# A graph and attention layer on one core: the mask products cut into four 64x64 pieces, and the mask made one step sooner

## The reference

```python
xn = _layernorm(x)
# sparse attention over the edges
x_norm = _layernorm(xn, ln_g, ln_b)
q, k, v = (x_norm @ Wq + bq), (x_norm @ Wk + bk), (x_norm @ Wv + bv)     # as (N, H, HD)
scores = jnp.einsum('ehd,ehd->eh', q[origin], k[destination]) * SCALE
ws = scores * edge_weights
e = jnp.exp(ws - seg_max[origin])
att = e / (denom[origin] + 1e-16)
values = segment_sum(att[:, :, None] * v[destination], origin)
gnn = xn + (values @ W1 + b1) @ W2 + b2
# linear attention mixer on the same xn, then a small table-like block
x = x + gnn + mix(xn)
x = x + ffn(_layernorm(x))
```

## Time and profile before

| what | value |
|---|---|
| median of 3 runs | 853.5 us (851.43 to 857.59) |
| the profiled execution, device time | 854.37 us |
| its span in the trace | 851.2 us |
| busy: TensorE, VectorE, ScalarE, GpSimd | 92%, 69%, 40%, 54% of the span |
| chain that ended last, by engine | PE 70%, DVE 21%, DMA 4% |
| attention loop, from the first scores | about 365 us to the end |
| granted TensorE clock, mean | 0.98 |

### The profile page before, as it was taken

The page is one execution under the profiler, slowest core; times in us unless marked ns, Lnnn a source line. Parts: engine busy times, 40 slices in busy tenths (PEclk is TensorE's granted clock), DMA queues, the critical chain, the costliest instruction groups (busy, mean ns, idle before and its releaser), DMA issues.

```text
span 851.2 us, 13484 instructions
## 1 busy us (share of the span) xinstructions
PE 782.4 (92%) x4751; PEld 458.3 (54%) x4791; DVE 583.2 (69%) x1331; ACT 339.6 (40%) x794; POOL 457.5 (54%) x391
## 2 busy tenths in 40 slices
PE   2999897899999999979999999999999999999993
PEld 2554445444446444435555555555556667666661
DVE  3487594954233503358888888998988978878886
ACT  0311301022312122035556555556555555545662
POOL 1028878778778877777777787777610001001000
PEclk9989999998999999979999999999999999999998
DMA  7697968897546569315353535435354143242203
GB/s 225 175 375 269 320 203 277 250 357 227 161 136 200 158 185 335 95 15 193 103 202 104 185 120 160 146 103 193 108 164 165 66 152 104 95 148 89 86 1 120
DMA packets 69632, 143.98 MB, mean 169 GB/s; under 512 B 20537, under 2 KB 54251, under 8 KB 65599
## 3 DMA queue, kind: packets, MB, share of 16 engines
q1 hardware_dynamic: 47084, 119.42, 39.9%
q0 software_dynamic: 13344, 6.28, 6.6%
q10 hardware_dynamic: 9136, 17.39, 6.2%
HBM read 77.99 MB, written 64.77 MB: 168 GB/s over the span
## 4 chain that ended last, share of the span: by engine, by line
PE 70%; DVE 21%; DMA 4%; issue 3%; ACTq 1%; ACT 1%; DVEq 0%
PE bank L890 17%; PE bank L884 12%; DVE AR L1540 11%; PE bank L1118 8%; PE bank L1085 8%; PE bank L1100 8%; PE bank L1090 4%; PE bank L1147 4%; DVE AR L1549 3%; DMA AR<-w_tab 2%; PE bank L998 2%; PE bank L873 1%; DMA AR<-in_L_gnn_b_dram 1%; PE bank L987 1%; PE bank L949 1%
## 5 line engine op out<-in xcount | busy, mean ns | idle before, releaser
L514 POOL DMA_INDIRECT w_tab<-pay,idx x330 | 403.9, 1224 | 153.3 <-issue 153.0
L765 ACT ACTIVATE AR<-AR,nmx 128x512 f32<-128x512 f32 (+1 forms) x240 | 159.0, 664 | 48.0 <-DVE nmx L1544 46.5
L1540 DVE CUSTOM_DVE_ANT_0 AR<-bank,AR,MX 128x512 f32<-128x512 f32 (+1 forms) x160 | 151.8, 986 | 20.0 <-PE bank L1090 19.1
L772 ACT ACTIVATE AR<-bank 128x512 f32<-128x512 f32 (+1 forms) x120 | 67.3, 561 | 173.9 <-PE bank L1100 173.9
L1085 PE MATMUL bank<-KT,QT 64*128 64x512 f32 (+1 forms) x480 | 118.3, 570 | 8.6 <-issue 5.3
L1100 PE MATMUL bank<-ident,AR 128*128 128x128 f32 (+2 forms) x880 | 122.7, 280 | 1.1 <-ACT AR L765 1.1
L1118 PE MATMUL bank<-AR,V 128*64 128x128 f32 (+1 forms) x1600 | 114.0, 280 | 6.1 <-DVE AR L1549 6.0
L884 PE MATMUL bank<-AR 128*128 128x512 f32 (+1 forms) x288 | 109.0, 538 | 7.3 <-ACT QT L642 3.2
L1118 PEld LDWEIGHTS bank<-AR,V 128*64 128x64 f32 (+1 forms) x1600 | 85.6, 136 | 52.3 <-issue 50.9
L890 PE MATMUL bank<-AR 128*128 128x512 f32 x240 | 108.3, 607 | 2.5 <-ACT AR L696 2.5
L1100 PEld LDWEIGHTS bank<-ident,AR 128*128 128x128 f32 (+2 forms) x880 | 94.0, 139 | 22.3 <-issue 15.9
(11 more groups left out here) (250 smaller groups left out, 755.2 us busy)
## 6 DMA issues: line engine op xcount, KB each, us to landing
w_tab<-ztile SPq DMA_DIRECT2D x20, 2280.0 KB, 15.0
AR<-w_tab SPq DMA_DIRECT2D x20, 2048.0 KB
AR<-w_tab SPq DMA_DIRECT2D x10, 1344.0 KB
w_tab<-ztile SPq DMA_DIRECT2D x3, 1800.0 KB, 13.2
w_tab<-pay,idx POOLq DMA_INDIRECT x330, 4.4
w_tab<-ztile SPq DMA_DIRECT2D x2, 1700.0 KB, 16.5
kv_rows<-AR ACTq DMA_DIRECT2D x9, 256.0 KB, 6.5
kv_rows<-V ACTq DMA_DIRECT2D x9, 256.0 KB
```

The source lines that it names most:

```text
L514: pool.indirect_dma_start(out=w_tab, out_offset=bass.IndirectOffsetOnAxis(ap=idx[:, k, j:j + 1], axis=0), in_=pay[:, k % RING, j, :], in_o ...
L765: act.activation(ws[u % 2][hh][:, 0:n], ws[u % 2][hh][:, 0:n], ACT.Exp, bias=nmx[:, u % 4, hh:hh + 1], accum_out=DG[g][:, c, 2 * p + hh:2 ...
L772: act.activation(PT[u % 2][0][:, 0:nb * P], bank[2][:, 0:nb * P], ACT.Copy).then_inc(s_ea, 1)
L1540: v.tensor_tensor_reduce(out=ws[u % 2][hh][:, 0:n], in0=bank[SB[(2 * u + hh) % 3]][:, 0:n], in1=Wt[w % 2][:, 0:n, h], scale=1.0, scalar=MX ...
```

## The change

It touches four places. On TensorE the mask of one head is now two products of 64x64 instead of one of 128x128, four for the two heads of a unit. The even head uses the rows 0 to 63 of the array, the odd head the rows 64 to 127, each once for the lower and once for the upper half of the output partitions. Two of the four need the mask's other half of partitions in their rows of the array, and so a second copy of the mask, `pens`, with exchanged halves. SyncE makes that copy by two DMAs of 64 partitions a tile (`swap_halves`), into the free buffers of two bias rows. TensorE waits for it at `p == 0` between the score and the mask products. VectorE makes `mask(w+1)` at `p == 1`, behind `merge`, and no longer at `p == 2`.

```diff
+        pens = [bias_row[1 + i][:, 0:256].bitcast(BF16) for i in range(2)]
...
+            def swap_halves(w):
+                n = GROUPS[w // NT][1]
+                sp.wait_ge(s_pen, w + 1)
+                if w >= 2:
+                    sp.wait_ge(s_s, 4 * (w - 1))
+                for i in range(2):
+                    sp.dma_start(pens[w % 2][64 * i:64 * i + 64, 0:n], pen[w % 2][64 - 64 * i:128 - 64 * i, 0:n]).then_inc(s_pens[w % 2], 16)
+
+            load_tile(0)
+            load_tile(1)
             for w in range(NW):
-                load_tile(w)
+                swap_halves(w)
+                if 1 <= w < NW - 1:
+                    load_tile(w + 1)
...
+                if p == 0:
+                    pe.wait_ge(s_pens[w % 2], 32 * (w // 2 + 1))
                 for hh in range(2):
-                    last = mm(bs[hh][:, 0:n], identb[:, :], pen[w % 2][:, 0:n], start=False, stop=True)
+                    for to in range(2):
+                        a, b = 64 * hh, 64 * to
+                        last = mm(bs[hh][b:b + 64, 0:n], identb[a:a + 64, a:a + 64], (pen if hh == to else pens)[w % 2][a:a + 64, 0:n], start=False, stop=True)
...
                 if w >= 2:
                     dve.wait_ge(s_s, 4 * (w - 1))
+                    dve.wait_ge(s_pens[w % 2], 32 * (w // 2))
...
-                if p == 2 and w < NW - 1:
+                if p == 1 and w < NW - 1:
                     mask(w + 1)
```

More of the change, by code:

```diff
@@ L339, in gps_layer @@
         s_pen = sem("mask_ready")
+        s_pens = [sem(f"mask_halves_swapped{i}") for i in range(2)]
         s_s = sem("scores_ready")
```

## The result

The changed kernel takes **858.2 us** (median of 20 executions; 850.9 to 863.6), the kernel before 853.5 (of 20; 851.0 to 857.6): 1.0048 times as long, 95% interval 1.0025 to 1.0071. The forecast was 851.3, a little faster, with a range of 842 to 863. The time lies in the range, but on the other side of the time before.

What follows compares the result with a forecast made beforehand. TensorE bounds tiles up to 10, a TensorE-VectorE chain the later ones. Terms -6.4 (group 0, tile 10), +2.0 (group 1), +2.0 (group 2), +0.2 (slow load) give -2.2: from 853.5 to 851.3 us, range 842 to 863.

Steps and rivals of the forecast that it cites:

- The gain of group 0: Eleven attention tiles: four units a tile each save 0.16 us, less 0.06 a tile waiting for the load; -6.4 us.
- Part 1: TensorE's mask phase: four quarter products run at once, so it costs one product instead of two; 0.16 us saved a unit.
- s: Saving per unit in TensorE's mask phase: 0.16 us, bounds 0.13 and 0.22; 0.08 in the tiles from 20 on.
- group 2: Attention tiles 20 to 29, bound by a TensorE-VectorE chain; forecast +0.22 us a tile from the earlier mask.
- Rival B: TensorE's mask phase: only pairs of products run at once, 0.06 us longer than now; +14 us, 867.5; chance 0.13.
- rival A: Attention loop: TensorE is the bound throughout and the mask's place costs nothing; 15.7 us less, 837.8; chance 0.12.
- group 1: Attention tiles 11 to 19, bound by a TensorE-VectorE chain; forecast +0.22 us a tile from the earlier mask.
- Part 2: VectorE's earlier mask: covered by idle time in tiles up to 10, inside the chain in later ones, +0.22 us a tile.
- Part 3: Mask waiting for its tile's table load: 0.06 us a tile up to tile 10, and +0.2 for one slow load.
- rival C: Tiles up to 10: loads landing later than 8 us bind the mask; at 9.5, +8 us, 857 to 861; chance 0.09.
- the load beside the gathers: Table load issued at 620.69, just after GpSimd's row gathers begin; the mask's wait for it, +0.2 us, bounds -1.3 and +2.5.
- Part 4: SyncE's two DMAs a tile for the exchanged mask copy: hidden, no cost; 1 to 2 us once if uncovered at the start.

Runs made afterwards that it cites:

- two_shift: Kernel before with the mask at p == 1, plus 16 tiny products ahead of TensorE's attention loop; 923.2 us, in a session with the kernel before at 922.9.
- after_again: The changed kernel itself, untouched, run once more as a control in the fourth session; 899.4 us, ratio 1.046 to the kernel before.
- four_late: The changed kernel with the mask put back to p == 2, four products and exchanged copy kept; 852.07 us, ratio 0.9983 to the kernel before.

## Why the prediction was wrong

Two terms failed. The gain of group 0, forecast at -6.4 us, came to -1.5, because the wait for the load was priced at 0.06 us a tile and the scatter was not in the sum at all. And what lies behind a late load, the idle TensorE and its low clock, was priced at nothing. The two mechanisms that the forecast was built on, the four products and the mask inside the chain, were right.

**Part 1, four products at a time: right, size off.** They run together; s is 0.20 (0.12 in group 2) where I had 0.16 (0.08). The difference of 0.04 fits the loads: I counted the 136 ns load of the values for the 64-column loads of the mask, and they take 104. That was a misreading too: the 136 ns row is of fp32 weights, the 97 ns row of bf16, so the two do not show what narrowing a load costs, and do not bear out the restriction on narrow loads as the forecast has it. The packing part of the Trainium skill's page "TensorE: Matmul & The Clock Gate" would have given 0.21, an estimate, and the traces agree with it (0.20). Rival B (only pairs) is out, and rival A (TensorE the bound throughout) by the chain: tiles of group 1 got longer.

Three sums of the forecast come out otherwise when they are redone with its own terms: s at its bounds, with group 2's saving moved along, gives -7.0 and +0.2 (not -6.6 and -0.2), the change loses below s = 0.13 (not 0.12), and s = 0.21 gives -6.2 (not -5.8). The forecast of -2.2 itself stands; the room for a loss was a little wider than stated.

**Part 2, the mask inside the chain: right.** Forecast +0.22 us a tile in both groups; measured +0.14 and +0.13, the difference being the larger s. Eighteen tiles cost 2.4 us by these, not 4.0.

**Part 3, the load: this step failed, twice.** First, "I take 0.06 a tile, bounds 0 and 0.5": the masks waited 7.2 us in the ten tiles, and each of these gained 0.15 us instead of 0.80. The 7.7 us that I read from one load was the time of a load with the fetch at its end. The slack was nil, I had seen that, and I priced the wait as if landing times were a constant of the load. In the trace after they take one of two values, 7.2 to 7.6 and 8.2 to 9.0, by where the instruction fetch falls, and this change moves the fetches. The trace before had one late load too (tile 2, 8.4 us), which a list of all of them would have shown. It was rival C, with another traffic than the one named there, and between its 9.5 and my 7.9: the page gives 8.8 as the median from issue to landing. That the fetch is the cause rests on 248 loads of which all but five sort by it, and on `two_shift`, which moved it; no kernel held it apart from everything else.

Second, "+0.2, bounds -1.3 and +2.5" for the load beside the gathers: the wait grew from 1.25 to 2.82 us, inside the bounds, but I had no price for what an idle TensorE brings: 3.53 us idle, and 6.8 us at half the clock. +3.9 us in that stretch (3.6 without its two chain terms), 4.7 against the same kernel without the collision, where the kernel before paid 1.15. The low clock at the end wasn't foreseen either; what brings it stays open, and another profile of the same kernel (`after_again`) has none of it ahead of the last stretch. Over 20 executions of the changed kernel the time goes with the mean granted clock, 7.8 us for each 0.01; its mean was 0.974, that of 29 executions of the kernel before in the first session 0.978, where the same slope is 3.8. That puts 1.6 to 3.3 of the 4.7 us between the medians beside the clock, an estimate from the two slopes; a wait lengthens the time and lowers the clock at once, so it doesn't say which came first.

**Part 4, the exchanged copy: right** with the mask at `p == 1`: no wait for it in the trace after, and leaving it out moved the tiles of group 1 by nothing. `four_late` shows that the earlier mask is what hides it.

**Left out of the sum: the scatter.** Even with all loads in time, the changed kernel could have been only 2.4 to 2.9 us ahead at the end of tile 10, and not 6.4, since the load of tile 10 waits for the last scatter of its half and the mask at `p == 1` waits for that load. This bound took 3.5 to 4 us of the forecast 6.4; the late loads took 1 us more, down to the measured 1.6. A sum with both right (-2.4 to -2.9 for group 0, +2.4 for the chains, +0.2 for the gathers) would have said "no change" and still missed the clock.

| term | forecast | measured |
|---|---|---|
| group 0, tile 10 and start | -6.4 | -1.6 |
| group 1 and 2, chains | +4.0 | +2.2 |
| load beside the gathers | +0.2 | +3.6 |
| end | 0 | +2.9 |
| sum, of the span | -2.2 | +7.1 |

## What to carry to other kernels

Before an edit spends the last of a buffer's slack, list the landing times of all its loads, not of one, and ask which small traffic falls into the late ones; here the instruction fetches moved with the instructions that were added to the loop. When a stage is to gain several microseconds, look for what starts the next stage: here a scatter on GpSimd held the first load of group 1, and with the mask early in the tile most of the gain could not pass it. A mask one step later could have waited for that load at half the price, so the same edit that uses up the slack also makes the floor felt. Price a wait of TensorE of several microseconds by more than its length: here a mask that waited 2.8 us, with half the clock behind it, cost 4.7.

A version that looks better than both was found but never measured undisturbed: four products with the mask on ScalarE, with tiles of 15.09 and 16.06 us against 15.49 and 16.30 before. By these it would be 9 x 0.40 + 9 x 0.24 = 5.8 us below the kernel before; that is an estimate from the tiles of groups 1 and 2 alone, and no run has shown it.

## What the runs showed of the hardware that I had not expected

- A 2 MB load with a 16 KB instruction fetch (0.9 to 1.3 us) inside it ended 1.2 us later than one without, 8.2 to 8.5 us behind the issue instead of 7.0 to 7.5 (266 loads of 19 profiles).
- With three gathers of whole rows, issued 1.4 us apart just ahead of it, such a load ended at 11.9 us, and at 8.2 in the same kernel where they lay 42 us ahead.
- Four products of 64x64 with 512 columns in the four quarters of the array start within 0.01 us and take 0.34 us start to start, beside 0.54 for two full-array products of the same columns.
- Semaphore signals of TensorE came some 2 us late (between 380 and 560 us the copy of the transposed probabilities began 1.5 to 3.1 us behind the transposes' end in the median of each of 14 profiles, and 0.04 in six others) through whole sessions, while GpSimd ran its scatters. The changed kernel took 858 us in one session and 899 in another, and the kernel before 854 and 904.
